# Two residual convolution blocks: output sums written in place of the relu's result, 4 KB store packets, image quarters loaded and stored one at a time

## What is computed

```python
def _quantize_per_tensor(t):
    s = jnp.max(jnp.abs(t))
    q = jnp.clip(jnp.round(t * (MAXV / s)), -MAXV, MAXV)
    return (q, s)
...
def _L0_conv_ref(x, weight, bias):
    qx, sx = _quantize_per_tensor(x)
    qw, sw = _quantize_per_tensor(weight)
    out = lax.conv_general_dilated(qx, qw, window_strides=(1, 1), padding=((1, 1), (1, 1)), dimension_numbers=('NCHW', 'OIHW', 'NCHW'))
    out = out * (sx * sw / (MAXV * MAXV))
    return out + bias.reshape(1, -1, 1, 1)
...
    h = _instnorm_lrelu(_disco_conv(image, weight1))
    return _instnorm_lrelu(_disco_conv(h, weight2))
...
x = x + _L0_conv_ref(_gn(x), L0_conv_weight, L0_conv_bias)
x = x + _L1_conv_ref(_gn(x), L1_conv_weight1, L1_conv_weight2)
```

## Time and profile before

| | before |
|---|---|
| median of 3 runs | 389.74 us (388.55 to 390.42) |
| the profiled execution, its own time | 387.53 us |
| its span, first to last instruction | 385.7 us |
| granted clock of PE, mean of the span | 0.94 |
| busy: PE, DVE, ACT, POOL | 66%, 68%, 56%, 50% |
| DMA: read, written | 36.38 MB, 16.78 MB |

### The profile page before, as it was taken

How to read it: one execution, slowest core, us unless ns; L and a number is a source line. 1 busy time by engine, 2 the same in 40 slices (tenths; PEclk the granted TensorE clock), 3 DMA queues, 4 the chain that set the end, 5 groups by cost and what they waited for, 6 DMA issues and landing times.

```text
span 385.7 us, 14732 instructions
## 1 busy us (share of the span) xinstructions
PE 255.3 (66%) x6752; PEld 141.3 (37%) x6752; DVE 260.5 (68%) x407; ACT 215.7 (56%) x191; POOL 194.6 (50%) x242
## 2 busy tenths in 40 slices
PE   0000100348689985998778988979688998698920
PEld 0000100323244542455335634624353573384500
DVE  2698898758887780977376637947493995255753
ACT  1059997580052436636653764397059637667772
POOL 0488867293402542925872586368338135442550
PEclk9999999999899998999896969998999999899965
DMA  7999904910840191266556244795744124304377
GB/s 261 358 428 422 358 0 109 290 42 2 221 106 5 28 228 31 46 169 132 167 126 161 78 145 112 177 340 136 202 103 137 37 63 126 97 16 122 112 219 217
DMA packets 83326, 59.09 MB, mean 153 GB/s; under 512 B 6848, under 2 KB 82080, under 8 KB 82080
## 3 DMA queue, kind: packets, MB, share of 16 engines
q1 hardware_dynamic: 83264, 58.15, 51.4%
HBM read 36.38 MB, written 16.78 MB: 138 GB/s over the span
## 4 chain that ended last, share of the span: by engine, by line
DVE 29%; PE 24%; DMA 15%; ACT 14%; issue 7%; SPq 5%; POOL 4%; DVEq 0%; POOLq 0%
PE ring L1084 17%; DVE bn_c L927 8%; DMA xs<-xa_dram 8%; DVE amax L849 6%; PE ring L1047 5%; DMA xs<-xb_dram 4%; DVE bn_x L917 4%; ACT c2one L523 3%; DVE spread_x L809 3%; ACT xs L523 2%; DVE xs L907 2%; ACT xs L508 2%; SPq L386 2%; ACT live L508 2%; DMA live<-xb_dram 2%
## 5 line engine op out<-in xcount | busy, mean ns | idle before, releaser
L927 DVE BATCH_NORM_STATS2 bn_c<-ring 128x6 f32<-128x512 f32 x128 | 79.6, 684 | 58.4 <-PE ring L1084 58.3
L1084 PE MATMUL ring<-hpad,w12t 32*32 32x512 f32 x2560 | 99.9, 631 | 5.6 <-ACT hpad L502 2.4
L502 ACT COPY hpad<-ring 128x1024 f32<-128x1024 f32 x32 | 32.3, 1015 | 65.8 <-DVE bn_c L927 65.8
L1084 PEld LDWEIGHTS ring<-hpad,w12t 32*32 32x32 f32 x2560 | 52.6, 105 | 38.2 <-issue 17.4
L1084 PE MATMUL ring<-xs,w1s 32*32 32x512 f32 x1280 | 49.2, 653 | 9.8 <-issue 5.8
L1084 PE MATMUL ring<-live,w1s 32*32 32x512 f32 x1280 | 45.7, 597 | 6.7 <-issue 6.1
L1047 PE MATMUL ring<-qpad,w0t 64*32 64x512 f16 x1344 | 42.9, 410 | 5.0 <-DVE qpad L898 2.5
L515 ACT ACTIVATE hpad<-hpad,params 128x1536 f32<-128x1536 f32 (+1 forms) x24 | 35.0, 1526 | 12.6 <-POOL params L631 12.6
L1084 PEld LDWEIGHTS ring<-xs,w1s 32*32 32x32 f32 x1280 | 27.0, 107 | 30.8 <-issue 22.8
L508 ACT ACTIVATE xs<-xs,single 128x1024 f32<-128x1024 f32 x16 | 17.5, 1150 | 31.2 <-DMA xs<-xb_dram 31.2
L622 POOL TENSOR_SCALAR var_eps<-moments_c 128x1 f32<-128x1 f32 x16 | 3.1, 192 | 60.3 <-DVE moments_c L824 59.7
(11 more groups left out here) (105 smaller groups left out, 377.7 us busy)
## 6 DMA issues: line engine op xcount, KB each, us to landing
xs<-xa_dram SPq DMA_DIRECT2D x8, 2048.0 KB, 10.0
live<-xb_dram SPq DMA_DIRECT2D x16, 512.0 KB, 7.1
xs<-xb_dram SPq DMA_DIRECT2D x16, 512.0 KB, 7.2
out_dram<-live SPq DMA_DIRECT2D x16, 512.0 KB, 4.4
out_dram<-xs SPq DMA_DIRECT2D x16, 512.0 KB, 4.4
hpad<-xa_dram SPq DMA_DIRECT2D x1, 2048.0 KB, 8.8
live<-live SPq DMA_DIRECT2D x8, 192.0 KB, 4.1
xs<-xs SPq DMA_DIRECT2D x8, 192.0 KB, 4.1
```

The source lines that it names most:

```text
L502: nc.scalar.copy(to, pair_of(g, n)).then_inc(taken[v], 1)
L927: ins = nc.vector.bn_stats(bn[f"c{v}"][:, QUADS * g + k, :], ring[:, bank_of(g, k), :])
L1084: ins = nc.tensor.matmul(ring[C * c:C * (c + 1), bank_of(g, r), :].rearrange("p (y x) -> p y x", x=IMG), w, window(v, b, r, c, g, dy, dx), ...
```

## The change

`output` on POOL and DVE adds `x1_of(t)` to the relu's result and writes the sum over it, in `c2_of(t)`. `store` reads there, so that a partition's share of a quarter is one run of 4096 bytes. An x1 quarter is free when its sum is done, so `load_xb` waits for POOL's count, quarter by quarter, and the four loads of an image stand in four places of SP's order. `c2_of(t)` is free only when image t - 2 is stored, so ACT's copy waits for that. Each half of a load has its own semaphore; ACT's bias stands earlier; the fourth quarter's relu and sum go behind the next copies. The quarters are taken in the order 0, 2, 1, 3. Images 2 and 3 are loaded earlier, DVE makes both halves of the first sum before its statistics, and `KEEP_Q` goes from 40 to 64.

```diff
--- before.py
+++ after.py
@@ -29,7 +29,7 @@
 GN_MEMBERS = 2 * QUADS
 IN_MEMBERS = QUADS
 
-KEEP_Q = 40
+KEEP_Q = 64
 
 MAXV = 127.0
 ROUND = 12582912.0
@@ -226,7 +226,7 @@
         w12_in = sem("w12_in")
         x_in = [sem(f"x_in{b}") for b in range(B)]
         x_in_again = sem("x_in_again")
-        xb_in = [sem(f"xb_in{b}") for b in range(B)]
+        xb_in = [[sem(f"xb_in{b}_{h}") for h in range(2)] for b in range(B)]
         w0_step = sem("w0_step")
         wmax_done = sem("wmax_done")
         products_done = sem("products_done")
@@ -307,7 +307,7 @@
 
 
         ROW_SETS = [slice(0, CHUNK, CHUNK - 1), slice(1, HALF), slice(HALF, CHUNK - 1)]
-        BIAS_ORDER = (0, 2, 1, 3)
+        PIECES = (0, 2, 1, 3)
 
         gn_tiles = [flat(live[1])[:, 0:COLS], c2one[:], flat(live[0])[:, 0:COLS]]
 
@@ -379,12 +379,12 @@
                     sp.wait_ge(low_pool, low_pool_count(2, 0))
                 elif b < LIVE:
                     sp.wait_ge(q_pool, 4 * (b - 2))
-                if b >= LIVE:
-                    sp.wait_ge(stored_of[b - LIVE], 16 * QUADS)
-                for n in of:
-                    n = BIAS_ORDER[n]
+                for k in of:
+                    if b >= LIVE:
+                        sp.wait_ge(out_pool, QUADS * (b - LIVE) + k + 1)
+                    n = PIECES[k]
                     sp.dma_start(inner(x1_of(b))[:, n], grid(xb_d[b, :, n * PIECE:(n + 1) * PIECE])
-                                 ).then_inc(xb_in[b], 16)
+                                 ).then_inc(xb_in[b][k // 2], 16)
 
             def write_share(t):
                 sp.wait_ge(stat_step["c2"], t + 1)
@@ -395,56 +395,65 @@
                 sp.dma_start(share[:, :, 1:3], stat_d.unsqueeze(0).to_broadcast([QUADS, C, IN_MEMBERS, 2])
                              ).then_inc(shared, 16)
 
-            def store(t, n):
+            def store(t, k):
                 if t == B - 1:
-                    sp.wait_ge(out_dve, 2 + n + 1)
-                elif t == B - 2 and n < 2:
-                    sp.wait_ge(out_dve, n + 1)
+                    sp.wait_ge(out_dve, 2 + k + 1)
+                elif t == B - 2 and k < 2:
+                    sp.wait_ge(out_dve, k + 1)
                 else:
-                    sp.wait_ge(out_pool, QUADS * t + n + 1 - (2 if t == B - 2 else 0))
-                sp.dma_start(grid(out_d[t, :, n * PIECE:(n + 1) * PIECE]), inner(x1_of(t))[:, n]
-                             ).then_inc(stored_of[t], 16)
+                    sp.wait_ge(out_pool, QUADS * t + k + 1 - (2 if t == B - 2 else 0))
+                n = PIECES[k]
+                sp.dma_start(out_d[t, :, n * PIECE:(n + 1) * PIECE], piece(c2_of(t), n)).then_inc(stored_of[t], 16)
 
             load_xb(0)
             load_xb(1)
             q_edges(0)
             q_edges(1)
+            load_xb(2)
             x1_edges(0)
-            load_xb(2)
             x1_edges(1)
             q_edges(2)
+            load_xb(3)
             for t in range(B - 2):
+
+                late = LIVE <= t + 3 < B
                 if t >= 1:
                     write_share(t - 1)
-                if t >= 1 and t + 3 < B:
-                    load_xb(t + 3, (0, 1))
+                if late:
+                    load_xb(t + 3, [2])
                 if t >= 1:
                     read_share(t - 1)
                 h_edges(t)
-                if t >= 1 and t + 3 < B:
-                    load_xb(t + 3, (2, 3))
+                if t == 1:
+                    load_xb(t + 3)
+                if late:
+                    load_xb(t + 3, [3])
                 x1_edges(t + 2)
-                if t == 0:
-                    load_xb(3)
+                if t >= 2:
+                    store(t - 2, 0)
+                    store(t - 2, 1)
+                    sp.wait_ge(conv_done[1], 2 * (t + 1) + 1)
+                    store(t - 2, 2)
                 if t == 3:
                     sp.wait_ge(q_pool, 4 * (5 - 1))
                     sp.dma_start(x_again(B - 1), xa_d[B - 1, :, :]).then_inc(x_in_again, 16)
                 if t + 3 < B:
                     q_edges(t + 3)
-                if t >= 1:
-                    for n in range(QUADS):
-                        store(t - 1, n)
+                if t >= 2:
+                    store(t - 2, 3)
+                if LIVE <= t + 4 < B:
+                    load_xb(t + 4, [0])
+                    sp.wait_ge(conv_done[2], 2 * t + 1)
+                    load_xb(t + 4, [1])
             write_share(B - 3)
             read_share(B - 3)
             h_edges(B - 2)
-            store(B - 3, 0)
-            store(B - 3, 1)
+            for k in range(QUADS):
+                store(B - 4, k)
             h_edges(B - 1)
-            store(B - 3, 2)
-            store(B - 3, 3)
-            for t in (B - 2, B - 1):
-                for n in range(QUADS):
-                    store(t, n)
+            for t in (B - 3, B - 2, B - 1):
+                for k in range(QUADS):
+                    store(t, k)
             for t in range(B):
                 sp.wait_ge(stored_of[t], 16 * QUADS)
 
@@ -494,7 +503,7 @@
                     if v == 2 and t == 1:
                         act.wait_ge(q_pool, 4 * (4 - 1))
                     if v == 2 and t >= 2:
-                        act.wait_ge(out_pool, QUADS * (t - 1))
+                        act.wait_ge(stored_of[t - 2], 16 * QUADS)
                 if v == 1:
                     to = by_chunk(hpad[t % 2])[:, n::2, HALF * g:HALF * (g + 1), :]
                 else:
@@ -502,9 +511,9 @@
                 nc.scalar.copy(to, pair_of(g, n)).then_inc(taken[v], 1)
 
             def add_bias(b, of=(0, 1, 2, 3)):
-                act.wait_ge(xb_in[b], 16 * QUADS)
-                for n in of:
-                    x = inner(x1_of(b))[:, BIAS_ORDER[n]]
+                for k in of:
+                    act.wait_ge(xb_in[b][k // 2], 32)
+                    x = inner(x1_of(b))[:, PIECES[k]]
                     nc.scalar.activation(x, x, ACT.Identity, bias=bias[:]).then_inc(biased, 1)
 
             def make_h(t, n):
@@ -515,11 +524,11 @@
                 nc.scalar.activation(rows, rows, ACT.Prelu, bias=param(shift["c1"], t), scale=param(scale["c1"], t),
                                      alpha=SLOPE).then_inc(h_ready, 1)
 
-            def norm_out(t, n):
-                if n == 0:
+            def norm_out(t, k):
+                if k == 0:
                     act.wait_ge(norm_ready["c2"], t + 1)
                     act.wait_ge(taken[2], QUADS * (t + 1))
-                y = piece(c2_of(t), n)
+                y = piece(c2_of(t), PIECES[k])
                 nc.scalar.activation(y, y, ACT.Prelu, bias=param(shift["c2"], t), scale=param(scale["c2"], t),
                                      alpha=SLOPE).then_inc(out_norm, 1)
 
@@ -541,21 +550,23 @@
                     take(2, t - 1, 1, 1)
                 for n in range(3):
                     make_h(t, n)
+                if t + 3 < B:
+                    add_bias(t + 3, (0, 1))
                 take(1, t + 1, 0, 0)
                 take(1, t + 1, 0, 1)
+                if t + 3 < B:
+                    add_bias(t + 3, (2, 3))
                 if t >= 1:
                     norm_out(t - 1, 0)
                 take(1, t + 1, 1, 0)
                 take(1, t + 1, 1, 1)
                 if t >= 1:
-                    for n in range(1, QUADS):
-                        norm_out(t - 1, n)
-                if t + 3 < B:
-                    add_bias(t + 3, (0, 1))
+                    norm_out(t - 1, 1)
+                    norm_out(t - 1, 2)
                 take(2, t, 0, 0)
                 take(2, t, 0, 1)
-                if t + 3 < B:
-                    add_bias(t + 3, (2, 3))
+                if t >= 1:
+                    norm_out(t - 1, 3)
             t, z = B - 2, B - 1
             take(2, t - 1, 1, 0)
             take(2, t - 1, 1, 1)
@@ -716,10 +727,10 @@
                 nc.gpsimd.tensor_scalar(bands(qpad)[:, n * CHUNK:(n + 1) * CHUNK, :], grid(low_of(b, n)), 1.0, 0.0,
                                         ALU.mult, ALU.add).then_inc(q_pool, 1)
 
-            def output(t, n):
-                pool.wait_ge(out_norm, QUADS * t + n + 1)
-                x = inner(x1_of(t))[:, n]
-                nc.gpsimd.tensor_tensor(x, x, grid(piece(c2_of(t), n)), ALU.add).then_inc(out_pool, 1)
+            def output(t, k):
+                pool.wait_ge(out_norm, QUADS * t + k + 1)
+                y = grid(piece(c2_of(t), PIECES[k]))
+                nc.gpsimd.tensor_tensor(y, inner(x1_of(t))[:, PIECES[k]], y, ALU.add).then_inc(out_pool, 1)
 
             pool.wait_ge(max_done, B + 1)
             zero_bands(q_one).then_inc(q_border, 1)
@@ -743,6 +754,8 @@
                 scale_taps(t + 1)
                 frame(t + 1)
                 normalise("c1", t)
+                if t >= 2:
+                    output(t - 2, 3)
                 if t + 3 < B:
                     for n in range(4):
                         to_low(t + 3, n)
```

(12 more changed lines are left out.)

## The result

The changed kernel takes 362.37 us in the median (359.19 to 365.31); the kernel before, run beside it, 389.36 (388.55 to 390.42). The ratio is 0.9278 with a 95% interval of 0.9205 to 0.9351. The ratios, here and in the table of experiments, leave out runs that lay over 1.5% above the fastest of the same kernel; the medians do not. Foretold were 366.0 us and 354 to 379. The profiled execution took 363.34 us (foretold: 363.8), its span is 361.4 (foretold: 362.0).

The account below looks back on a forecast made before the run. The prediction took a chain of waits through ACT's copy, not a busy engine, to bound the kernel. Its terms summed to -23.7 us: 362.0 of span, 363.8 for that execution, 366.0 for the median, range 354 to 379.

Parts of the forecast that it names:

- Ahead of the loop: Before the first period: earlier loads of images 2 and 3 end idle waits, less part of a bias: -2.5 us.
- Whether the clock rises sooner no row shows ... I take 0: 24 more idle products before the quantised convolution: an earlier clock rise could give at most 3.5 us, counted as 0.
- the ends given for the loads: Limits of the term before the first period: -6 from idle PE and the bias's share, +1 from loads beside instruction packets.
- Periods of t = 1 to 4: Loop periods, 145.29 us together before: changes of -1.5, -5.9, -2.8 and -5.2 us, to 33.5, 31.7, 33.0 and 31.7.
- The step that leaves 1.1 us of a halt in t = 2 and 4: One load quarter issued where two stood ahead of a 3.2 us PE halt, so a third of it remains.
- Rival 1: PE's halts stay, being unrelated to loads or because quarters still go out bunched: +8.3 us, 374.3; chance 0.22.
- The floor of 29.39 us: Measured period of t = 5, without image loads or biases, taken as the least a loop period can take.
- signs of being wrong: ACT idle before conv 2's first copy, released by a store, or before a bias; 3 us halts; gathers 35 us apart.
- rival 3: Slower: ACT's first conv 2 copy waits for image t - 2's fourth store; 398 at 8 us lateness; chance 0.06.
- Behind the loop: After the last gathers: -2.2 us from one POOL sum moved behind `frame`, -1.0 from faster products after the shorter wait.
- Stores: Last four stores at the end: 4 KB runs land faster than 512-byte rows, the last after 3.4 us: -2.0 us.
- The small product: DVE's product at L809 in the loop falls from 2.10 to 0.18 us once POOL's sum moves behind it.

Follow-up runs that it names:

- e7_act_old: Changed kernel with ACT's biases and its fourth relu quarter all back at their old places: 367.58 us, ratio 0.9426.
- e1_keep40: Changed kernel with 40 idle products (`KEEP_Q`) instead of 64: 370.30 us, ratio 0.9540.
- e2_loads_late: Changed kernel with images 2 and 3 loaded at their old places in the order of the DMAs: 375.22 us, ratio 0.9628.
- e12_best: Changed kernel with image 4 and third quarters loaded earlier, 2 MB reread behind the fourth store, image 3's bias before the loop, another POOL sum behind edges: 351.55 us.
- e10_waits: Changed kernel with biases of t = 0, 1 back about conv 2's copies, image 4 loaded earlier, 2 MB reread behind the fourth store: 358.39 us.
- e5_store512: Changed kernel with its stores in pieces of 512 bytes, the result's rows in another order on the device: 370.19 us, ratio 0.9471.
- e3_bias_late: Changed kernel with ACT's biases at their old places, about the copies of conv 2: 361.37 us, ratio 0.9284.
- e9_one_sem: Changed kernel in which each ACT bias again waits for all four quarters of its image: 376.25 us, ratio 0.9715.

## Why the prediction was right, and where not

**The bound** was read rightly: a chain through ACT's copy, not a busy engine. The gathers no longer wait for it, and with ACT's old order four of five do again (e7_act_old).

**Ahead of the loop: -2.5 foretold, -8.05 measured.** The step that failed is "Whether the clock rises sooner no row shows ... I take 0". Its own bound of 3.5 us was about the truth: 3.8 us by e1_keep40. The rest, some 4.2 us, lies inside the ends given for the loads (-6 to +1), but that it was the loads is not shown. By the earlier gathers 6.45 us were already gained (115.56 to 109.11), 3.1 of them with the 24 products (112.20 in e1_keep40), and with both loads late (e2_loads_late) these gathers hardly moved. Image 3's load is a condition for the rest of the way. No run undoes the other moves ahead of the loop together, so the cause of some 3 us stays open.

**Periods of t = 1 to 4: -15.4 foretold, -12.4 measured.** The direction held in all four, and t = 4 gave 1 us more than said. The step that leaves 1.1 us of a halt in t = 2 and 4 failed: the halts fell in length, not in sum, 11.60 us in t = 2 to 4 after 10.47 before. Spreading the quarters over the period spread the halts over it; leaving the loads out (4.23 us) or issuing them earlier (7.63 us) lowers them. What came instead is PE's pace: 8.3 us less busy time in these three periods, where the prediction had 2.3 us of slow products behind one halt. Shorter halts and the higher granted clock came together; no run isolates the one from the other. Rival 1's first half, "the halts stay", came true in this sense, but not its reason: they do depend on the loads. The floor of 29.39 us was none: e12_best went 1 us below it.

**Waits that take the place.** ACT idle before a bias, and before a copy of conv 2 released by a store, were signs of being wrong, and both came. At t = 1 the bias ahead of the copies cost PE 3.47 us of the 4.1 that the prediction put there, and the 256 products behind it another 1.6 (10.30 us against the 8.73 that such a group takes at a granted clock of 1.00). At t = 3 rival 3's mechanism was there, once: ACT waited 5.32 us for the fourth store, behind the 2 MB read, as that term's reason had it, but PE only 0.28; with the read behind the store (e10_waits) the wait was gone and the period 0.6 us shorter. At t = 0 the bias cost 3.45 us, inside the term ahead of the loop.

**Behind the loop: -3.2 foretold, -1.2 measured** (the -3.49 less 2.3 of stores). PE's timeline after:

```profile
309.43 11.96 PE L1099 MATMUL ring<-xs,w1s 32*32 32x512 f32 x312 [2.08 <-POOL xs L669]
```

The wait fell by 1.4, from 3.49 us, not by 2.2: POOL's sums now start 2.40 us ahead of the gathers (302.05) where they had 3.14. And the granted clock still fell, to a mean of 0.51 from 310.5 to 314; the 1.0 us for it was not there. The 217 products of the earlier trace rows are those that start before 340 us; the whole group, 311 products, took 11.88 us before, and 312 take 11.96 now.

**Stores: -2.0 foretold, -2.3 measured** (5.4 to 3.1). The two rates of the earlier trace rows had told against the rule of line rate from 512 bytes in the Trainium skill's "DMA: Bandwidth & Descriptors", section "Specifications"; e5_store512, with pieces of 512 bytes, tells against it too: 5.6 us against 3.1.

**The small product** takes 0.18 us in t = 1 to 4, as foretold, and e3_bias_late shows that its 2.1 us lie mostly in slack.

**What no term covered**: the semaphore for each half. In the new order its undoing costs 13.9 us, more than any term of the sum.

So the total was close by luck: too small a term ahead of the loop made up for the halts that stayed and the tail. The 2.21 us added for the median did not come either: the median lies 0.97 us below the profiled execution.

## What to carry to other kernels

Undo an order's moves together before calling one of them worthless: late biases alone and an early relu quarter alone showed no cost clear of the noise, both together made the gathers wait for ACT again, with a median 6 us higher. An edit that looks like plumbing, such as a semaphore for half a transfer, can be what makes the order run, so ask of each wait what stands behind it when it counts all the pieces. And when traffic is spread out to shorten a stall, add the stall up over the period; here it went from few long halts to many short ones. Then count the products behind a stall as well: here a wait of 3.45 us was followed by products that took 1.5 us longer.

## What was not expected of the hardware

- The granted clock was 0.61 behind 40 idle products and 2.81 us without work, and 1.00 behind 64 and 1.76 us; that is worth about 4 us.
- Behind waits of 3.45 and 3.47 us for ACT the next 256 products took 10.23 and 10.30 us, at a mean granted clock of 0.83; behind a wait of 1.34 us (e3_bias_late) they took 8.73 at 1.00. It is not so every time: in e9_one_sem they took 8.73 us behind a wait of 3.41.
- PE's halts at the ends of instruction packets follow the loads: 11.60 us with the loads of three images, 4.23 without them.
- The same 512 KB stored in pieces of 4 KB rather than 512 bytes land 3.1 instead of 5.6 us after the issue when four follow each other, and SP issues each in 0.33 instead of 0.53 us.
